# Cross attention in a decoder layer: one set of scores, exponentials turned on TensorE, in place of two sets of scores

## What is computed

```python
def proj(x, W, b):                       # 16 heads of 32
    y = x @ W.T + b
    return y.reshape(B, -1, NUM_HEADS, D_K).transpose(0, 2, 1, 3)
q, k, v = proj(query, Wq, bq), proj(key, Wk, bk), proj(value, Wv, bv)
scores = jnp.einsum('bhqd,bhkd->bhqk', q, k) / jnp.sqrt(jnp.float32(D_K))
attn = jax.nn.softmax(scores, axis=-1)
ctx = jnp.einsum('bhqk,bhkd->bhqd', attn, v)
...
x = x + _L0_attn_ref(_layernorm(x, axis=-1), ...)
x = x + _L0_xattn_ref(_layernorm(x, axis=-1), ctx_1024, ctx_1024, ...)
x = x + _L0_ffn_ref(_layernorm(x, axis=-1), ...)
```

## Time and profile before

| | us |
|---|---|
| median of the runs | 2458.64 (2458.32 to 2460.63) |
| span of the profiled execution | 2453.0 |
| TensorE matmul busy, share | 2350.3, 96% |
| VectorE busy, share | 1349.7, 55% |
| ScalarE busy, share | 1049.9, 43% |
| GpSimd busy, share | 791.4, 32% |
| first matmul of cross attention | 744.61 |
| first matmul of the experts | 1209.34 |

### The profile page before, as it was taken

One profiled execution on the slowest core, in us unless ns is written; L12 is line 12 of the kernel. 1 busy time (PEld: TensorE's weight loads), 2 busy tenths in 40 slices (PEclk: granted clock), 3 DMA queues, 4 the chain that ended last, 5 costly groups with the idle time before them and its releaser, 6 DMA issues.

```text
span 2453.0 us, 33616 instructions
## 1 busy us (share of the span) xinstructions
PE 2350.3 (96%) x12584; PEld 1779.7 (73%) x12584; DVE 1349.7 (55%) x2168; ACT 1049.9 (43%) x1893; POOL 791.4 (32%) x754
## 2 busy tenths in 40 slices
PE   7999998999997999999799999999999999999998
PEld 6888885566665465555578878888888888888887
DVE  5555456777764455554654557444564445644444
ACT  3556566776741333333354445333343333433332
POOL 1444454433330122223577764111111111111111
PEclk9999999999996999999899999999999999999999
DMA  7655447666637344452456544654346444464442
GB/s 203 167 135 146 113 104 189 202 191 176 187 113 181 83 117 120 149 149 92 171 173 210 183 157 178 209 176 145 125 141 212 174 138 136 139 207 137 137 140 83
DMA packets 129553, 379.60 MB, mean 155 GB/s; under 512 B 14736, under 2 KB 37008, under 8 KB 110864
## 3 DMA queue, kind: packets, MB, share of 16 engines
q1 hardware_dynamic: 128848, 376.70, 49.9%
q10 hardware_dynamic: 544, 0.75, 0.1%
HBM read 246.20 MB, written 103.81 MB: 143 GB/s over the span
## 4 chain that ended last, share of the span: by engine, by line
PE 49%; DVE 1%; issue 0%; ACT 0%; DVEq 0%
PE ex_pg L2653 31%; PE ex_pd L2669 17%; DVE ex_xb L2470 0%; PE ex_pd L2619 0%; DVE ex_up L2490 0%; PE ex_pd L2630 0%; DVE ex_acc L2507 0%; ACT ex_xb L2320 0%; DVE stage L2466 0%; DVE ex_ht L2499 0%; DVE ex_lg L2408 0%; DVE ex_rank L2442 0%; DVE ex_rank L2441 0%; DVE ex_gt L2439 0%; DVE ex_rank L2440 0%
## 5 line engine op out<-in xcount | busy, mean ns | idle before, releaser
L2653 PE MATMUL ex_pg<-ex_xb,first_wg 128*128 128x512 f32 x3360 | 820.6, 391 | 12.7 <-DVE ex_up L2490 7.4
L2653 PEld LDWEIGHTS ex_pg<-ex_xb,first_wg 128*128 128x128 f32 x3360 | 631.3, 188 | 153.4 <-issue 16.4
L2669 PE MATMUL ex_pd<-ex_wd,ex_ht 128*128 128x512 f32 x1920 | 486.4, 389 | 2.9 <-issue 2.6
L2669 PEld LDWEIGHTS ex_pd<-ex_wd,ex_ht 128*128 128x128 f32 x1920 | 360.0, 188 | 79.1 <-issue 4.5
L2507 DVE SCALAR_TENSOR_TENSOR ex_acc<-ex_pd,ex_share,ex_acc 128x512 f32<-128x512 f32 x320 | 239.6, 749 | 302.4 <-PE ex_pd L2669 302.2
L2327 ACT COPY ex_m<-ex_pg 128x512 f32<-128x512 f32 x240 | 140.8, 586 | 383.6 <-PE ex_pg L2653 383.4
L2271 POOL TENSOR_TENSOR ex_h<-ex_g,ex_up 128x512 f32<-128x512 f32 x80 | 103.3, 1291 | 553.3 <-issue 469.4
L425 POOL TENSOR_TENSOR pr_ks_sum<-pr_ks_sum,pr_kp 128x512 f32<-128x512 f32 x128 | 165.1, 1290 | 161.7 <-DVE pr_kp L573 150.7
L2331 ACT ACTIVATE ex_g<-ex_g 128x512 f32<-128x512 f32 x160 | 101.2, 632 | 238.0 <-DVE ex_g L2483 165.6
L2263 POOL TENSOR_TENSOR ex_wd<-stage,ex_wd 128x512 fp32r<-128x512 f32 x80 | 105.5, 1342 | 260.1 <-ACT ex_wd L2308 260.1
L1572 ACT ACTIVATE cr_ring<-cr_s_bank 128x512 f32<-128x512 f32 x160 | 89.2, 602 | 162.6 <-PE cr_s_bank L1869 135.2
(11 more groups left out here) (225 smaller groups left out, 3439.1 us busy)
## 6 DMA issues: line engine op xcount, KB each, us to landing
first_wg<-w_scratch SPq DMA_DIRECT2D x60, 1024.0 KB, 5.1
first_wg<-w_scratch SPq DMA_DIRECT2D x60, 768.0 KB, 4.4
w_scratch<-first_wg SPq DMA_DIRECT2D x20, 1792.0 KB, 6.8
stage<-in_units SPq DMA_DIRECT2D x60, 512.0 KB, 6.9
qk<-pr_kq SPq DMA_DIRECT2D x192, 128.0 KB, 2.4
qk<-q_scratch SPq DMA_DIRECT2D x96, 256.0 KB, 4.8
cr_q<-xq_scratch SPq DMA_DIRECT2D x96, 256.0 KB, 5.4
q_scratch<-pr_kq SPq DMA_DIRECT2D x128, 128.0 KB, 2.3
```

The costliest lines, as they stand in the source:

```text
L2653: mm = nc.tensor.matmul(pg[f][BANK[j]][:], wg[:, f, j, s, c * P:(c + 1) * P], xb[:, j, m, c * TB:(c + 1) * TB], start=(k == 0 and j in FRESH),
L2669: mm = nc.tensor.matmul(bank_of("D", n, i)[:], ht[:, s, f, k, t * P:(t + 1) * P], wd[:, n % 2, m, f * D:(f + 1) * D], start=(at == 0), sto ...
```

## The change

The scores are made once, with tokens on partitions (`scores`, the matmul of line 1841 before), group after group (`n` from 0 to 31). VectorE reduces each bank to minus its maxima (`top`). ScalarE takes the exponential of each head's 154 columns with that as its bias, and has the instruction's sum output write the denominator (`den`): 16 instructions of 154 columns per group in place of 5 of 512. The factor of the softmax is now multiplied into the key weights, one VectorE operation in the linear stage. `prob` holds each head's 154 exponentials in consecutive elements. TensorE transposes them (`turn_weights`), 4 of 128x128 per head, and 4 more for the rests of four heads, which GpSimd copies together first (`place_rests`). ScalarE copies two of the five turned banks of a group to `ring`, VectorE three. Numerators are made as before. Denominators by matmul, the maxima's way into the queries and the spreading by matmul are gone. In their place VectorE inverts a block's 64 denominators per token, TensorE turns them in four transposes, ScalarE copies them, SyncE writes them to memory and reads them back, each row to 32 partitions (`spread_rec`). The multiplication, the high part and the low part move to GpSimd, except in the last block. The numerators are now copied by VectorE, not ScalarE. x is loaded and stored by tile, not by block. Output projection of tile m comes five groups later, its transposes six. Banks are now three for scores, two for turned weights, two for the rest, one for numerators; queries' ring is 3 groups.

The core of the diff:

```diff
+    SBANKS, TBANKS, BANKS = 3, 2, 2
+    ON_ACT = (0, 3)
+    ON_DVE = (1, 2, 4)
+    O_LAG, T_LAG = 5, 6
+    STEPS = range(-1, N + T_LAG)
...
+                def spread_rec(i):
+                    sp.wait_ge(act_read, ACT_AT[("R", i)])
+                    sp.dma_start(rec_dram[i], rec_row[:]).then_inc(row_out, 16)
+                    sp.wait_ge(row_out, 16 * (i + 1))
+                    if i:
+                        sp.wait_ge(divided, TT * i)
+                    rows = rec_dram[i].rearrange("(g j) t -> j g t", j=HG)
+                    for j in range(HG):
+                        sp.dma_start(rec[j * HD:(j + 1) * HD], rows[j:j + 1].broadcast_to([HD, G, TB])).then_inc(rec_in, 16)
...
+                    pool.wait_ge(s_read, MU * (n + 1))
+                    nc.gpsimd.tensor_copy(rest_w[:, :, :, 0:KREM], prob[:, n % 2, :, :, P:KEYS]).then_inc(rests_set, 1)
...
+                for n in range(N):
+                    if live(n - T_LAG):
+                        reciprocal_std(n - T_LAG)
+                    place_rests(n)
+                    if live(n - 4):
+                        normalise(n - 4)
+                        add_bias(n - 4)
+                        normalised_high(n - 4)
+                        normalised_low(n - 4)
...
+                def weights(n, v):
+                    i, g = n // G, n % G
+                    if n >= 2 and v == 0:
+                        act.wait_ge(t_full, SU * (n - 1))
+                    act.wait_ge(top_set, MU * n + v + 1)
+                    for at, (t, j) in enumerate(PIECES[v]):
+                        last = nc.scalar.activation(prob[:, n % 2, t, j, 0:KEYS],
+                                                    s_bank[(MU * n + v) % SBANKS][:, at * KEYS:(at + 1) * KEYS], ACT.Exp,
+                                                    bias=top[:, n % 2, t, j:j + 1],
+                                                    accum_out=den[:, i % 2, t, g * HG + j:g * HG + j + 1])
+                    last.then_inc(s_read, 1)
...
+                def maximum(n, v):
+                    dve.wait_ge(s_full, MU * n + v + 1)
...
+                def turned_weights(n, j):
+                    if n >= 2:
+                        dve.wait_ge(num_full, n - 1)
+                    dve.wait_ge(t_full, SU * n + j + 1)
+                    nc.vector.tensor_copy(ring[:, n % 2, j], t_bank[(SU * n + j) % TBANKS][:]).then_inc(t_dve, 1)
...
+                def turn_weights(n, j):
+                    at = SU * n + j
+                    if at >= TBANKS:
+                        pe.wait_ge(*t_taken((at - TBANKS) // SU, (at - TBANKS) % SU))
...
+                    for t in range(TT):
+                        src = prob[:, n % 2, t, j, 0:P] if j < HG else rest_w[:, t].rearrange("p j k -> p (j k)")
+                        mm = nc.tensor.transpose(t_bank[at % TBANKS][:, t * P:(t + 1) * P], src, ident[:])
+                    mm.then_inc(t_full, 1)
...
+                for n in STEPS:
+                    ahead, now, out = live(n + 1), live(n), live(n - O_LAG)
+                    if ahead:
+                        scores(n + 1, 0)
+                    if now:
+                        turn_weights(n, 0)
+                    if live(n - 1):
+                        heads(n - 1)
+                    if ahead:
+                        scores(n + 1, 1)
+                    if now:
+                        turn_weights(n, 1)
+                    if live(n - 1):
+                        rests(n - 1)
+                    if ahead:
+                        scores(n + 1, 2)
+                    if now and n % G == G - 1:
+                        turn_reciprocals(n // G)
+                    if out:
+                        out_proj(n - O_LAG, 0, 6)
+                    if now:
+                        turn_weights(n, 2)
+                    if ahead:
+                        scores(n + 1, 3)
+                    if out:
+                        out_proj(n - O_LAG, 6, 12)
+                    if now:
+                        turn_weights(n, 3)
+                    if ahead:
+                        scores(n + 1, 4)
+                    if live(n - T_LAG):
+                        transposes(n - T_LAG)
...
+                    if now:
+                        turn_weights(n, 4)
+                    if ahead:
+                        scores(n + 1, 5)
```

More of the change, by code:

```diff
@@ L1294, in attend_cross @@
-    ACT_AT = {JOBS[n]: at + 1 for at, n in enumerate(ON_ACT)}
+    ACT_AT, DVE_AT = {}, {}
+    for key in JOBS:
+        at = ACT_AT if key[0] in ("T", "R") else DVE_AT
+        at[key] = len(at) + 1
     with ExitStack() as ctx:
@@ L1586, in normalised @@
-                def normalised(i, groups=range(G)):
-                    for g in groups:
-                        act.wait_ge(dve_read, DVE_AT[(i, "R", g)])
-                        nc.scalar.copy(u[:, HI, g], num[:, g]).then_inc(norm_hi, 1)
-                def turned(i, tiles=range(TT)):
-                    for t in tiles:
-                        if t == 0 and i:
-                            act.wait_ge(x3_out, 16 * i)
-                        elif t == 0:
-                            for out in xq_out:
-                                act.wait_ge(out, 32 * NBLK)
-                        act.wait_ge(filled, POS[(i, "T", t)] + 1)
-                        nc.scalar.copy(x3[:, :, t * P:(t + 1) * P],
-                                       bank_of(i, "T", t)[:].rearrange("p (c n) -> p c n", c=C)).then_inc(act_read, 1)
@@ new lines, in turned @@
+                def turned(m):
+                    if m % TT == 0 and m:
+                        act.wait_ge(x3_out, 16 * (m // TT))
+                    act.wait_ge(filled, POS[("T", m)] + 1)
+                    nc.scalar.copy(x3[:, :, tile_cols(m)], bank_of("T", m)[:].rearrange("p (c n) -> p c n", c=C))\
+                        .then_inc(act_read, 1)
+                act.wait_ge(ctx_in, 32)
+                for g in range(G):
+                    context(0, g)
+                act.wait_ge(dve_read, DVE_AT[("CK", 0, G - 1)])
@@ new lines, in _ @@
+                dve.wait_ge(bk_set, 1)
+                for g in range(G):
+                    context_keys(0, g)
+                for n in range(2):
+                    context_values(0, n)
+                for n in range(-1, N):
+                    ahead, now = live(n + 1), live(n)
+                    if ahead:
+                        maximum(n + 1, 0)
+                    if live(n - T_LAG):
+                        norm(n - T_LAG)
+                    if ahead:
+                        maximum(n + 1, 1)
+                    if now and n % G == G - 1:
+                        reciprocal(n // G)
+                    if now:
+                        turned_weights(n, 1)
+                    if ahead:
+                        maximum(n + 1, 2)
+                    if live(n - 1):
+                        take_num(n - 1)
+                    if now:
+                        turned_weights(n, 2)
+                    if ahead:
+                        maximum(n + 1, 3)
+                    if n == 2:
@@ L1780, in _ @@
-                    add_out(i - 1, 3)
-                    moments(i - 1, 3)
-                    if FETCH(i):
-                        context_keys(i // BLK + 1, (2, 3))
-                    norm(i - 1, 2)
-                    norm(i - 1, 3)
-                    if FETCH(i):
-                        context_values(i // BLK + 1)
+                    if ahead:
+                        maximum(n + 1, 4)
+                    if live(n - O_LAG):
+                        add_out(n - O_LAG)
+                    for key in fetch_jobs(n):
+                        (context_keys if key[0] == "CK" else context_values)(*key[1:])
```

921 lines of the change are left out of this document (380 added, 541 removed).

## The result

| | before | after |
|---|---|---|
| median of the runs, us | 2458.86 (2458.32 to 2460.63) | 2381.14 (2376.01 to 2383.88) |
| profiled span, us | 2453.0 | 2379.2 |
| first matmul of cross attention | 744.61 | 743.49 |
| first matmul of the experts | 1209.34 | 1135.28 |

What follows compares the result with a forecast made beforehand. TensorE's matmul work was taken to bound cross attention. Terms 769.6 + 52.5 + 271.4 + 15 + 25.9 gave 1134.4, 75 us less; with 1 for scaling, span 2379, plus 5.6 to the median: 2385 us, range 2360 to 2440.

Steps and rivals of the forecast that it cites:

- TensorE per group: Cross attention, work per group of four heads: 9.4 us plus 0.3 for changes of kind, 9.7 against 11.9 before.
- VectorE 8.1, ScalarE 8.3, GpSimd up to 7.3: Cross attention, busy us per group of the other three engines, claimed to fit into TensorE's 9.7.
- The slack of the chain: Scores, maximum, exponential, bank: closes with little slack, each bank free 0.5 to 1.5 us before TensorE wants it.
- Queries hidden: SyncE's query load stands behind the reciprocals' write wait, but asked one group ahead, so claimed to cost nothing.
- The turn of reciprocals 0.6 us late: Once per block, VectorE's reciprocal ends about 0.6 us after TensorE comes to it; the one wait found.
- The sum of the stage: Cross attention's start, groups, contexts and tail summed to 1134.4 against 1209.3 for the experts' start: 75 us less.
- The tail: End of cross attention, from last numerators through projection of four tiles to the experts: 25.9 us.
- The scaling of the key weights: Linear stage, one VectorE pass of 2048 columns beside TensorE's work: 2 us if uncovered, 1 put.
- (a): Rival, cross attention: ScalarE becomes the bound through dearer exponentials, 12.0 us per group, 2445 us, or some 2405; chance 0.19.
- (b): Rival, cross attention: chain of scores, maximum, exponential, bank has less slack; 1.2 us more per group, 2417 us; chance 0.13.
- (c): Rival, cross attention: TensorE's granted clock stays low, 19 us per group, about 2630 us, slower than before; chance 0.10.
- (d): Rival, cross attention: waits eat all of the 75 us, time within 0.2% of before; chance 0.04.

## Why the prediction was right, step by step

**TensorE per group: right.** 9.4 of work plus 0.3 for changes of kind was set; it is 9.50, or 9.6 with a quarter of the reciprocals' turn, 0.43 a block. The transposes cost 0.09 to 0.14, the mean 0.11 as taken (2.15 against 2.2). The numerators cost 0.25 more than in one run, since they now lie apart: that is what the changes of kind cost, and nothing else is visible. With the rests turned twice, four more cost 0.42.

**VectorE 8.1, ScalarE 8.3, GpSimd up to 7.3: right in their consequence.** Measured 8.0, 7.7 and 5.6. The exponential was put at 0.28 + 0.14 = 0.42 and is 0.28 + 0.09 = 0.37; 16 times that difference is 0.8 us, and 0.6 of it shows. The Trainium skill, "ScalarE: Activation LUTs", section "What ACT_TABLE_LOAD costs", gave an estimate of 0.32 for the exponential without the sum; the trace has 0.28 here, so the row stands.

**The slack of the chain: right.** No wait for a bank stands in the steady groups after. One score bank less costs 1.3 us a group, 2.15 us more on ScalarE 0.35.

**Queries hidden: wrong.** The sentence was that the load "is asked for one group ahead, so it is hidden". It is asked a group ahead in SyncE's program, but SyncE reaches it late, because the stores of x, of a block's norm and of the reciprocals' row wait in front of it for VectorE and ScalarE, and then a load needs 8.0 us from issue to landing (median; 5.4 before). The waits were 11.9 us, and the kernel with the earlier load gained 13.4. The step priced one wait on SyncE and not the three others that stand in front of the loads.

**The turn of reciprocals 0.6 us late: right in kind.** 0.55 to 1.25 us, in 3 of 8 blocks; in the others the wait for a query had given VectorE that time. With the queries early it shows in 7.

**The sum of the stage: right, with terms that cancel.** By the starts of TensorE's turns in the trace:

| | predicted, us | measured, us |
|---|---|---|
| to the first turned exponentials | 769.6 | 763.75 |
| groups 0 to 4 | 52.5 | 46.4 |
| groups 5 to 31 and contexts | 271.4 + 15 | 287.7 |
| from there to the experts | 25.9 | 37.4 |
| experts' first matmul | 1134.4 | 1135.28 |

These four differences are -5.9, -6.1, +1.3 and +11.5 us; that they cancel to 0.9 is luck. The step from the span to the time has one term more. The span was put at 2379 and is 2379.2, but 5.6 us were added to it, by the one pair of span and time before, where the pair after differs by 1.7. So the median came out 3.9 us under 2385.

The start is early because the keys' transfer, kept in the sum as 5.58 us of idle, shrank to 1.85. SyncE issues the keys no sooner (5.7 us after the stage's first matmul, 5.5 before), but their pieces of 80 KB take 3.1 us from issue to landing in place of 6.9. Three loads of queries are issued ahead of them, not six; that this is the reason is likely, but no run tests it. The first exponentials' latency was less than set, too: 6.6 us from the first scores to the first turn, not 8.

```profile
757.11 1.20 PE L1865 MATMUL cr_s_bank<-cr_k_w,cr_q 96*128 96x154 f32 x9 [1.85 <-DMA cr_k_w<-cr_num]
...
763.75 1.05 PE L1883 MATMUL cr_t_bank<-ident,cr_prob 128*128 128x128 f32 x4
```

In the earlier trace rows the first scores come at 761.64. Groups 0 to 4 were priced as if the clock stayed low; it was low in only part of them:

```profile
757.00:771.30 14.30, 11.39 (x63) 10.38 (x64) 8.97 (x16) 12.46 (x63) 0.53 (x1) 0.64 1.06 266
771.30:822.30 51.00, 42.20 (x286) 26.59 (x285) 31.25 (x54) 38.93 (x176) 11.22 (x13) 0.87 0.47 101
```

The main term holds nearly to the digit: the contexts take 14.8 us more than plain groups (3.4 + 3.4 + 8.0 over 9.5), so the other 27 take (287.7 - 14.8) / 27 = 10.11 where 10.05 was said. But it is 9.6 of work and 0.5 of waits and what follows them instead of 9.7 and 0.35.

The tail was 11.5 us too short. The terms missing are in the timeline:

```profile
1099.78 3.02 PE L1927 MATMUL cr_bank<-cr_wo,cr_u 128*128 128x512 f32 x12
1108.40 1.09 PE L1936 MATMUL cr_bank<-ident,cr_xn 128*128 128x128 f32 x4 [5.60 <-DVE cr_xn L1746]
1112.69 5.08 PE L1927 MATMUL cr_bank<-cr_wo,cr_u 128*128 128x512 f32 x12 [3.20 <-DVE cr_x L1729]
```

Five tiles are projected there, not four (3.0 us, since the projection comes five groups late and the last numerators come one step after their group). The last block's reciprocals go through memory, which had "most of a group" of cover elsewhere and has none here: VectorE stands for them, with the multiplication, the norm and the additions queued behind:

```profile
1106.50 1.29 DVE L1806 TENSOR_TENSOR cr_num<-cr_num,cr_rec 128x512 f32<-128x512 f32 x2 [3.69 <-DMA cr_rec<-rec_scratch]
```

And after 8.8 us of idle, with four transposes between, the clock is low for the next twelve matmuls, 5.08 us in place of 3.0, so 2 us more. The 3.0, the 3.7 and the 2 are 8.7 of the 11.5; what the other 2.8 are is not shown.

**The scaling of the key weights: no cost visible.** Cross attention starts at 743.49, 1.1 us earlier than before, not 1 us later; in the traces of the other kernels with the scaling it starts at 742.9 to 745.1, once at 747.6, so 1 us could hide in that spread.

**Rivals.** (a) didn't come: ScalarE has 1.8 us of room. (b) didn't come. (c), the clock, didn't come, for a better reason than the one given. The prediction leaned on the projection, "30% of the new group"; with the projection nearly gone the clock stayed at 1.00 for the 106 us in which TensorE didn't stand for long. What did bring low stretches were waits, and they passed. The prediction set beside this the Trainium skill, "TensorE: Matmul & The Clock Gate", section "Part 4: PE-mode transpose", by which transposes don't count as busy time for the clock in the way of other matmuls. In the kernel with two of twelve matmuls and early queries transposes are about 2.6 of TensorE's 7.1 us of work, and the clock is at 1.00 from 904 to 1010; no run here tests the rule by itself, and if it holds, it did not decide here. (d) didn't come: the time fell by 3.2%.

## What to carry to other kernels

When an engine's removed work is what bounds a stage, price the stage by that engine's distances between starts, then ask of every in-order queue, the DMA issuer's too, what stands in front of each load whose ring was made shorter; here that was 13 us and one line to mend. A sum that comes out right may hold terms that are 6 to 11 us off in both directions: check start, steady state and tail each by themselves, and in the tail look for latencies that the steady state had covered. To learn whether one thing holds the clock up, take the waits out first, since they bring it down by themselves.

## What the hardware showed that was not expected

- An exponential with a sum output is two instructions: the second, a read of the accumulator, has a record of 0.19 to 0.29 us (mean 0.215) and adds 0.09 from start to start.
- A product in one quarter of the array alone cost as much as four side by side in its four quarters: 0.96 us against 0.97, both ahead of full-width matmuls.
- The granted clock fell to 0.50 in or just behind TensorE's waits of 2.3 to 5 us, and the matmuls of the next few us ran at the lower level; so a wait can cost more than its length: with the 3.19 us wait at 1048 that group and the next take 24.4 us (13.07 + 11.31), and 20.1 with the queries early. In early groups without an output part, waits of 1.2 us in groups of 8.5 to 9.9 had one behind them at two places (779 and 789) and not at a third (798); in the kernel with two of twelve matmuls and early queries four of five such waits were not. What parts these is open.
- A GpSimd copy of 128x416 strided elements takes 535 ns, a quarter of it 335.
